# Score products of two heads in turn on two row strips of TensorE, with every engine's order rewritten, in a fused cross-attention and expert-layer kernel

## What is computed

```
h   = x + attention(layernorm(x), ctx, ctx)      # 16 heads of 8 features
out = h + ffn(layernorm(h))
scores = Q K^T / sqrt(8) + slope[head] * softplus(1000 + |i - j|);  softmax over j
ffn(y) = silu(y Sg) * (y Su) Sd  +  sum over the top 2 of 16 experts of  p_e * (silu(y Wg_e) * (y Wu_e)) Wd_e
```

## Time and profile before

| | us |
|---|---|
| median of three runs | 236.87 (236.17 to 238.17) |
| the profiled execution | 235.97 |
| its span, first to last instruction | 234.2 |
| between the two | 1.8 |

### The profile page before, as it was taken

One profiled execution on the slowest core, in us unless ns is written; L12 is line 12 of the kernel. 1 busy time (PEld: TensorE's weight loads), 2 busy tenths in 40 slices (PEclk: granted clock), 3 DMA queues, 4 the chain that ended last, 5 costly groups with the idle time before them and its releaser, 6 DMA issues.

```text
span 234.2 us, 6086 instructions
## 1 busy us (share of the span) xinstructions
PE 213.8 (91%) x1942; PEld 175.4 (75%) x1942; DVE 175.9 (75%) x612; ACT 118.3 (51%) x283; POOL 74.4 (32%) x178
## 2 busy tenths in 40 slices
PE   2969787979999999999999999999999899989995
PEld 2757455757788787977897878878897779768884
DVE  4599636995699678985899569957985788653891
ACT  8565656466426734475346443663367234763310
POOL 2500016010860159013921094107700580038000
PEclk9999999999999999999999999999999999999999
DMA  5553586223312470317032612325123600250000
GB/s 157 175 90 105 125 215 205 80 69 99 87 48 60 83 172 3 104 52 199 3 102 49 157 44 60 84 78 131 38 70 88 165 0 4 84 126 0 1 25 22
DMA packets 13079, 20.24 MB, mean 86 GB/s; under 512 B 2800, under 2 KB 9440, under 8 KB 12544
## 3 DMA queue, kind: packets, MB, share of 16 engines
q1 hardware_dynamic: 12080, 18.64, 31.2%
q10 hardware_dynamic: 976, 1.32, 1.8%
HBM read 16.03 MB, written 3.78 MB: 85 GB/s over the span
## 4 chain that ended last, share of the span: by engine, by line
issue 33%; PE 31%; DVE 17%; POOL 11%; ACT 3%; DMA 1%; DVEq 1%; ACTq 0%; POOLq 0%; SPq 0%
POOL hid L1314 6%; DVE nmax L971 6%; PE ps_up L511 5%; PE ps_pv L444 4%; PE ps_m L537 4%; PE ps_st L425 3%; PE ps_pv L451 3%; PE ps_up L516 2%; DVE tg L1075 2%; DVE stacks_sb L1202 1%; PE ps_up L308 1%; DMA ident<-in_c_ident 1%; DVE hid L1081 1%; PE ps_m L466 1%; POOL ve L1278 1%
## 5 line engine op out<-in xcount | busy, mean ns | idle before, releaser
L791 ACT ACTIVATE th<-ps_up 128x256 f32<-128x256 f32 x72 | 27.6, 383 | 35.5 <-PE ps_up L516 34.8
L735 ACT ACTIVATE probs<-ps_st 128x512 f32<-128x512 f32 x64 | 37.0, 595 | 16.3 <-PE ps_st L425 11.1
L537 PE MATMUL ps_m<-wd_sb,hid 128*128 128x128 f32 x288 | 44.8, 283 | 0.0
L971 DVE TENSOR_REDUCE nmax<-ps_s 128x4 f32<-128x512 f32 x64 | 41.9, 680 | 0.4 <-issue 0.4
L1075 DVE SCALAR_TENSOR_TENSOR tg<-th,ps_up 128x256 f32<-128x256 f32 x72 | 29.8, 414 | 13.5 <-ACT th L791 13.2
L1314 POOL TENSOR_TENSOR hid<-hid,crep 128x256 f32<-128x256 f32 x56 | 39.1, 732 | 0.2 <-issue 0.2
L537 PEld LDWEIGHTS ps_m<-wd_sb,hid 128*128 128x128 f32 x288 | 37.6, 191 | 1.0
L1081 DVE TENSOR_TENSOR hid<-tg,ps_up 128x256 f32<-128x256 f32 x72 | 29.7, 413 | 1.0
L511 PE MATMUL ps_up<-x_hi,wg_hi 128*128 128x256 f32 x72 | 26.6, 369 | 0.4 <-ACT x_hi L772 0.2
L1278 POOL TENSOR_TENSOR ve<-mv,eps_sb 128x1 f32<-128x1 f32 x16 | 3.0, 191 | 69.5 <-DVE mv L1022 69.5
L425 PE MATMUL ps_st<-stacks_sb 98*128 98x128 f16 x256 | 24.8, 220 | 0.2
(11 more groups left out here) (147 smaller groups left out, 434.2 us busy)
## 6 DMA issues: line engine op xcount, KB each, us to landing
crep<-cw_dram SPq DMA_DIRECT2D x28, 256.0 KB, 4.6
stacks_sb<-qk_dram SPq DMA_DIRECT2D x32, 128.0 KB, 3.4
qk_dram<-qk_parts SPq DMA_DIRECT2D x16, 128.0 KB, 1.8
out_y<-x_all SPq DMA_DIRECT2D x8, 128.0 KB, 4.6
wg_sb<-in_wgT ACTq DMA_DIRECT2D x1, 576.0 KB, 3.5
wu_sb<-in_wuT ACTq DMA_DIRECT2D x1, 576.0 KB, 3.3
wd_sb<-in_wd SPq DMA_DIRECT2D x1, 576.0 KB, 4.1
x_all<-in_x SPq DMA_DIRECT2D x2, 256.0 KB, 4.2
```

The source lines that it names most:

```text
L537: last = mm(ps_dn[:, b * P:(b + 1) * P], hid[:, buf, c, b * P:(b + 1) * P], wd_sb[:, c, :], start=(c == 0 and b == 0), stop=(c == SHARED), ...
L735: fn(probs[:, b, g * HG * P:(g + 1) * HG * P], scores_bank(a, g)[:], ACT.Exp).then_inc(exp_sb, 1)
L791: fn(th[:, c % 2, :], ps_up[c % 2][:, 0, :], ACT.Tanh, scale=0.5).then_inc(tanh_sb, 1)
L971: v.tensor_reduce(nmax[:, b, HG * g:HG * g + HG], ps_s[g % 2][:].rearrange("p (h j) -> p h j", h=HG), AX_X, ALU.max, negate=True).then_inc ...
```

## The change

- The stacks are laid out in two strips of 64 rows: heads 0 to 7 at row 0, heads 8 to 15 at row 64, each with 32 rows of features and, in the query stack, two rows of shifts (K: ones). Products take 32 or 34 rows from row 0 or row 64.
- `scores` and `scores_T` take a tuple of groups. i = 0 and 2 are heads 0 to 7, i = 1 and 3 are heads 8 to 15 (ORDER gives the group of heads: 0, 2, 1, 3). With two groups the products alternate between strips and banks, eight in a block. `first` passes single groups.
- In each step after the first attention, the biases of i = 0 and i = 2 of both halves come from SBUF: one copied by ACT, three by DVE (`seed(a, 1, 0)`, `seed(a, 0, 1)`, `seed(a, 1, 1)`). i = 1 computes its one bias product, i = 3 has none.
- SyncE issues the shift rows, two DMAs in place of one of ACT's, in order with its parts and stacks. The stacks are read with eight DMAs of half the size, in place of four. The zero fills of the stacks are gone, the `select` and `cwT_r` fills move to GpSimd.
- PE in a step: scores(0,(0,1)), q, k, down 0, down 1, expert_in_T, scores(0,(2,3)), down 2, up 0, down 3, up 1, scores(1,(0,1)), shift_T 0, router, up 2, scores(1,(2,3)), down 4, up 3, down 5, down 6, scores_T(0,(0,1)), up 4, shift_T 1, down 7, scores_T(0,(2,3)), up 5, down 8, weights_T, weigh_values 0, scores_T(1,(0,1)), up 6, values_T 0, scores_T(1,(2,3)), up 7, attention_T 0, weigh_values 1, and on as before.
- DVE in a step: row_max(0,0), (0,1), gate 8, hidden 8 of f - 1, x2_low, both qk_low, row_max(0,2), (0,3), max_high, max_low, gate 0, hidden 0, row_max(1,0), (1,1), gate 1, hidden 1, router_max, router_shift, gate 2, hidden 2, row_max(1,2), (1,3), max_high, route 0, max_low, route 1, seed(1,0), route 2, gate 3, route 3, hidden 3, route 4, norm1_stats, route 5, 6, seed(0,1), gate 4, norm1_mean, hidden 4, gate 5, hidden 5, seed(1,1), residual2, row_sums 0, normalise 0, gate 6, norm1, hidden 6, and on as before. In `first`, both qk_low stand after the second maximum of half 1 instead of behind the fourth.
- ACT in a step: as before to tanh 3, then exponential(0,0), (0,1), shift_copy 1, tanh 4, exponential(0,2), (0,3), tanh 5, weights_copy, values_copy 0, exponential(1,0), (1,1), tanh 6, exponential(1,2), (1,3), tanh 7, attention_copy 0, values_copy 1, and on as before.
- SyncE in a step: write_parts, shift_rows 0 (the other way round for group 0), stack_k, shift_rows 1, stack_q, then as before.
- `keep_clock` in `first`: 5 and 4 in place of 3 and 3 around scores(0,1,2).

The diff, cut to its core (context and the orders told above are left out):

```diff
@@ -39,9 +39,11 @@
+STRIP = 64
-ZROWS = 96
-AROWS = ZROWS + 2
+AROWS = SROWS + 2
+HS = H // 2
+ORDER = (0, 2, 1, 3)
...
@@ -112,13 +114,13 @@
-        stacks_sb = sb("stacks_sb", [AROWS, 2, 2, H, T], F16)
+        stacks_sb = sb("stacks_sb", [STRIP + AROWS, 2, 2, HS, T], F16)
-        nsplit = sb("nsplit", [P, NB, 2, H], F16)
+        nsplit = sb("nsplit", [P, NB, 2, 2, HS], F16)
...
@@ -223,23 +225,28 @@
-                    sp.wait_ge(act_pads, 1)
-                    sp.wait_ge(dve_pads, 2)
+            def stack_k(p, buf):
-                    src = bass.AP(qk_dram.tensor, (buf * 5 + plane) * (P * T), [[H * T, 2 * DH], [1, H * T]])
-                    sp.dma_start(stacks_sb[row:row + 2 * DH, buf, 1].rearrange("r h t -> r (h t)"), src).then_inc(s_stack, 16)
-                    sp.wait_ge(dve_pads, 1)
+                    for s in range(2):
+                        src = bass.AP(qk_dram.tensor, ((buf * 5 + plane) * P + s * HS) * T, [[H * T, 2 * DH], [1, HS * T]])
+                        at = STRIP * s + row
+                        sp.dma_start(stacks_sb[at:at + 2 * DH, buf, 1].rearrange("r h t -> r (h t)"), src).then_inc(s_stack, 16)
+            def stack_q(p, buf):
-                if not at_start(p):
-                    sp.wait_ge(s_nm[1], 16 * p)
-                    src = bass.AP(qk_dram.tensor, buf * 5 * (P * T), [[H * T, 2 * DH], [1, H * T]])
-                    sp.dma_start(stacks_sb[row:row + 2 * DH, buf, 0].rearrange("r h t -> r (h t)"), src).then_inc(s_stack, 16)
+                    for s in range(2):
+                        src = bass.AP(qk_dram.tensor, (buf * 5 * P + s * HS) * T, [[H * T, 2 * DH], [1, HS * T]])
+                        at = STRIP * s + row
+                        sp.dma_start(stacks_sb[at:at + 2 * DH, buf, 0].rearrange("r h t -> r (h t)"), src).then_inc(s_stack, 16)
+            def shift_rows(a, b, buf):
+                sp.wait_ge(nm_sb, 2 * a + b + 1)
+                for s in range(2):
+                    sp.dma_start(qs[buf][STRIP * s + SROWS:STRIP * s + AROWS, :, b * P:(b + 1) * P],
+                                 nmT[H * s:H * (s + 1), b, :]).then_inc(s_nm[b], 16)
...
@@ -257,24 +264,28 @@
             def load_more():
-                sp.wait_ge(s_nm[0], 16)
-                sp.wait_ge(s_nm[1], 16)
+                sp.wait_ge(s_nm[0], 32)
+                sp.wait_ge(s_nm[1], 32)
             def load_rest():
-                sp.wait_ge(s_stack, 128)
+                sp.wait_ge(s_stack, 256)
-                sp.wait_ge(dve_pads, 3)
+                sp.wait_ge(pool_pads, 2)
             def step(f, a, p, q, abuf):
-                if p is not None:
-                    stacks(p, 1 - abuf)
-                if a is not None and at_start(a): load_more()
+                if at_start(a): shift_rows(a, 0, abuf)
+                if p is not None: write_parts(p, 1 - abuf)
+                if not at_start(a): shift_rows(a, 0, abuf)
+                if p is not None: stack_k(p, 1 - abuf)
+                shift_rows(a, 1, abuf)
+                if p is not None: stack_q(p, 1 - abuf)
+                if at_start(a): load_more()
...
@@ -341,39 +354,36 @@
-            def scores(a, b, g, buf):
-                bank, n = ps_s[g % 2], 2 * NHG * a + NHG * b + g
-                if b == 0 and g == 0:
-                    pe.wait_ge(s_stack, 64 * a + 64)
+            def scores(a, b, groups, buf):
+                n = 2 * NHG * a + NHG * b
+                if b == 0 and 0 in groups:
+                    pe.wait_ge(s_stack, 128 * a + 128)
-                        pe.wait_ge(dve_pads, 1)
-                        pe.wait_ge(act_pads, 1)
-                    elif isinstance(a, int) and a == 1:
-                        pe.wait_ge(act_pads, 3)
-                elif b == 0 and g == 1:
+                if b == 0 and 1 in groups:
-                else:
-                    pe.wait_ge(max_sb, n - 1)
-                if g == 0:
-                    mm(bank[:], dist16[:], slope_hi[:, 0:HG, :], start=True, stop=False, skip_group_check=True)
-                for h in range(HG * g, HG * g + HG):
-                    o = (h - HG * g) * P
-                    last = mm(bank[:, o:o + P], qs[buf][0:ZROWS, h, b * P:(b + 1) * P],
-                              ks[buf][0:ZROWS, h, b * P:(b + 1) * P],
-                              start=(g > 0), stop=True, skip_group_check=True)
-                last.then_inc(s_mm, 1)
+                if b > 0 or groups[-1] > 1:
+                    pe.wait_ge(max_sb, n + groups[-1] - 1)
+                if 0 in groups:
+                    mm(ps_s[0][:], dist16[:], slope_hi[:, 0:HG, :], start=True, stop=False, skip_group_check=True)
+                for k in range(HG):
+                    for i in groups:
+                        row, h = STRIP * (i % 2), HG * (i // 2) + k
+                        last = mm(ps_s[i % 2][:, k * P:(k + 1) * P], qs[buf][row:row + SROWS, h, b * P:(b + 1) * P],
+                                  ks[buf][row:row + SROWS, h, b * P:(b + 1) * P], start=(i > 0), stop=True,
+                                  skip_group_check=True)
+                        if k == HG - 1:
+                            last.then_inc(s_mm, 1)
             def shift_T(a, b):
-                nc.tensor.transpose(ps_nm, nsplit[:, b, :, :].rearrange("p s h -> p (s h)"), ident16[:]).then_inc(nm_mm, 1)
+                nc.tensor.transpose(ps_nm, nsplit[:, b].rearrange("p t s h -> p (t s h)"), ident16[:]).then_inc(nm_mm, 1)
...
@@ -400,32 +410,38 @@
-            def scores_T(a, b, g, buf, f=None):
-                bank, n = scores_bank(a, g), 2 * NHG * a + NHG * b + g
-                seeded = not at_start(a) and (b, g) in ((0, 0), (1, 0), (1, 1))
+            def scores_T(a, b, groups, buf, f=None):
+                n = 2 * NHG * a + NHG * b
+                seeded = {i: not at_start(a) and i % 2 == 0 for i in groups}
-                if at_start(a) and (b, g) == (0, 1):
+                if at_start(a) and b == 0 and 1 in groups:
-                if seeded and b == 0:
-                    pe.wait_ge(seed0_sb, a)
-                elif seeded:
-                    pe.wait_ge(seed1_sb, 2 * a + g - 1)
-                elif not (at_start(a) and b == 0 and g < 2):
-                    pe.wait_ge(exp_sb, n - 1)
-                if g == 0:
-                    pe.wait_ge(s_nm[b], 16 * a + 16)
+                for i in groups:
+                    if seeded[i] and b == 0 and i == 0:
+                        pe.wait_ge(seed0_sb, a)
+                    elif seeded[i]:
+                        pe.wait_ge(seed1_sb, 3 * (a - 1) + 2 * b + i // 2)
+                if not (at_start(a) and b == 0 and groups[-1] < 2):
+                    pe.wait_ge(exp_sb, n + groups[-1] - 1)
+                if 0 in groups:
+                    pe.wait_ge(s_nm[b], 32 * a + 32)
-                first = False if seeded else bias(bank, g)[0]
-                for h in range(HG * g, HG * g + HG):
-                    o = (h - HG * g) * P
-                    last = mm(bank[:, o:o + P], ks[buf][:, h, b * P:(b + 1) * P], qs[buf][:, h, b * P:(b + 1) * P],
-                              start=first, stop=True, skip_group_check=True)
-                    first = False
-                last.then_inc(st_mm, 1)
+                    elif isinstance(a, int) and a == 1:
+                        pe.wait_ge(act_pads, 4)
+                first = {i: False if seeded[i] else bias(scores_bank(a, i), ORDER[i])[0] for i in groups}
+                for k in range(HG):
+                    for i in groups:
+                        row, h = STRIP * (i % 2), HG * (i // 2) + k
+                        last = mm(scores_bank(a, i)[:, k * P:(k + 1) * P], ks[buf][row:row + AROWS, h, b * P:(b + 1) * P],
+                                  qs[buf][row:row + AROWS, h, b * P:(b + 1) * P], start=first[i], stop=True,
+                                  skip_group_check=True)
+                        first[i] = False
+                        if k == HG - 1:
+                            last.then_inc(st_mm, 1)
...
@@ -740,10 +749,6 @@
-            def shift_rows(a, b, buf):
-                act.wait_ge(nm_sb, 2 * a + b + 1)
-                act.dma_start(qs[buf][ZROWS:AROWS, :, b * P:(b + 1) * P], nmT[:, b, :]).then_inc(s_nm[b], 16)
...
@@ -859,10 +860,8 @@
-            fill(stacks_sb[:, 0, 1], zero)
-            act.wait_ge(act_pads, 1)
-            act.wait_ge(dve_pads, 1)
-            fill(ks[0][ZROWS:AROWS], ones16)
+            for s in range(2):
+                fill(ks[0][STRIP * s + SROWS:STRIP * s + AROWS], ones16)
...
@@ -966,28 +965,30 @@
-            def row_max(a, b, g):
-                dve.wait_ge(s_mm, 2 * NHG * a + NHG * b + g + 1)
-                v.tensor_reduce(nmax[:, b, HG * g:HG * g + HG], ps_s[g % 2][:].rearrange("p (h j) -> p h j", h=HG), AX_X, ALU.max,
+            def row_max(a, b, i):
+                g = ORDER[i]
+                dve.wait_ge(s_mm, 2 * NHG * a + NHG * b + i + 1)
```

(14 more changed lines are left out.)

154 lines of the change are left out of this document (70 added, 84 removed).

## The result

| | before | after |
|---|---|---|
| median, us | 236.52 (236.0 to 238.17, four runs) | 248.72 (246.57 to 249.68, four runs) |
| the profiled execution | 235.97 | 246.57 |
| its span | 234.2 | 244.8 |
| PE's mean granted clock | 0.999 (the profiled execution) | 0.986, 0.979, 0.972, 0.972 (all four) |

What follows compares the result with a forecast made beforehand. PE, busy 91%, decides, with short waits mostly on DVE or ACT. Start-up +0.9, first step +0.8, middle steps +2.5, last +0.4 make +4.6 on 235.97: 240.6, predicted as 241.0; range 233.5 to 246, the forecast's own 237.5 to 244.5.

Steps and rivals of the forecast that it cites:

- the middle steps: Five middle pipelined steps: new orders and waits cost +0.5 us each, +2.5 in all.
- the start-up: First attention: half 1's shift rows land late behind SyncE's stack_k issues, +0.9 us, bounds 0 and +1.5.
- (a) to (c): PE work per middle step: strip pairs -1.66, shape switches +1.32, weight loads +0.30, fewer bias products -0.38; sum -0.42 us.
- points 1 to 7: Hand schedule of a middle step under the new orders, with PE's waits on other engines, summing to 25.46 us.
- point 5: Middle step: weights_T at T+15.70, ACT's 0.37 us copy at 16.13, weigh_values waiting for it until 16.55, before T+16.36.
- First step +0.8: First pipelined step: first L444 block 0.15 later and the same longer chain behind it, +0.8 us.
- rest +0.4: Last pipelined step, behind the middle ones: +0.4 us.
- A: Rival: reordered waits stay as large as before and PE's work decides, -0.42 a step, 233.1 us; chance 0.22.
- B: Rival: strips don't overlap, +1.66 us PE work a step over the forecast's, about half in waits, 247 us; chance 0.08.
- D: Rival: row strips switch free, at most -2.04 us a step, -14 in all, 222.6 us; chance 0.03.
- C: Rival: the steps' waits cost what PE saves, only the start-up's +0.9 is left, 237.8 us; chance 0.15.

Runs made afterwards that it cites:

- e3: Kernel after without strips: before's full-height stacks, zero fills and one shift DMA a half, all new orders and four seeds kept; 248.08 us, ratio 1.048.
- e4: Kernel before with score products taken from 64 rows instead of 96, giving them the strip shape without pairs; 242.20 us, ratio 1.024.
- e6: Kernel before with the bias of head group 1 of half 0 copied by ACT instead of computed by PE; 236.93 us, ratio 1.0005.
- e12: e3's kernel with e7's order, first attention's shift rows issued by ACT, shift_T(0,1) between the first two groups as before; 243.47 us, ratio 1.028.
- e5: Kernel before with the shift rows issued by SyncE at the change's places, one DMA each; 242.15 us, ratio 1.021.
- e14: Kernel after with e1's SyncE order, e7's order, and e13's DVE order and clock transposes in the first attention; 242.70 us, ratio 1.025.
- e1: Kernel after; in the first attention SyncE issues half 1's shift rows before stack_k, PE does shift_T(0,1) before the second scores_T group; 247.12 us, ratio 1.044.
- e10: Kernel after with keep_clock(14), transposes that compute nothing, ahead of scores_T(0, 0, (2,)) in the first attention; 247.88 us, ratio 1.041.
- e2: Kernel after with the loops of scores and scores_T exchanged: four products on one strip, then four on the other; 248.86 us.
- e13: e12's kernel with DVE's first-attention order as before (qk_low behind the last row maxima) and before's clock transposes; 240.33 us, ratio 1.017.
- e7: Kernel after with scores_T(1,(0,1)) ahead of weigh_values(0) on PE and exponential(1,0) ahead of values_copy(0) on ACT; 244.63 us, ratio 1.034.
- e8: Kernel after with the third seed written by ACT, and the routing weights' transposes and copy moved earlier; 245.84 us, ratio 1.038.
- e9: Kernel after with the first attention's shift rows issued by ACT, two DMAs a half; 248.26 us, ratio 1.047.
- e11: Kernel after with the changes of e7, e8 and e9 together; 248.48 us, ratio 1.048.

## Why the prediction was wrong

The direction and the main mechanism (waits made by the new orders) were right; the sum was 7.7 us short of the median. Two of its terms failed by 2.7 us each, the middle steps (+2.5 taken, +5.25 measured) and the start-up (+0.9 taken, +3.62 measured), and the granted clock was in no term. By its steps:

**PE's work, (a) to (c).** From windows, PE's busy time in a quick step went from 24.32 to 23.62, so -0.70, where I had -0.42. e3 splits it: 24.32 to 23.95 is the fourth seed, -0.37 (I had -0.38), and 23.95 to 23.62 the strips, -0.33 (I had -0.04). A pair costs as much as one product, as taken from L494 (pairs start 0.056 apart). The switches were priced too high: 13 of them are 1.09 in e4, where the same arithmetic gives 1.6. This error made the forecast too slow, if anything, by 0.3 us a step at most: e3 against after shows 0.33 us of PE work reach the time in full, e6 shows 0.25 reach it not at all.

**Waits, points 1 to 7.** The hand schedule held. Of the step that starts at 117.68, predicted and measured:

| | predicted, T+ | measured, T+ |
|---|---|---|
| scores(1,(0,1)) | 6.40 | 6.38 |
| seed(1,0) starts | 12.85 | 12.83 |
| up 5 | 14.53 | 14.49 |
| cw | 15.28 | 15.26 |
| weights_T | 15.70 | 15.75 |
| weigh_values 0 | 16.55 | 16.87 |
| from it to weigh_values 1 | 4.77 | 4.66 |
| from there to the end | 4.14 | 4.14 |
| step | 25.46 | 25.67 |

The one miss is point 5: the copy of cwT began 0.5 after the transposes (133.43 to 133.93), and weigh_values 0.25 behind its end.

**The sum was mis-sized where I chose.** "25.46 us, against a mean of 24.96. I take +0.5" set a schedule of the quick kind against the mean of both kinds. The quick kind was 24.65, so the schedule itself said +0.8, which I had named only as a bound. Measured is +1.05 a step, 5.25 instead of 2.5: 1.55 us from this choice, 1.05 from the 0.21 by which the schedule fell short of the measured step, the rest from the other kind of step.

**Start-up: +0.9 taken, 3.62 measured.** I had the second issue of half 1's shift rows at 26.3 and its landing at 28.4. It was issued at 27.56 and landed at 29.28. The step that failed is the time of SyncE's issues, not the 2 us from issue to landing, which were 1.72. Three things made them late. The stack reads wait for the second write of the parts (23.47 here, 24.68), 1.7 us behind it; I counted the 1.7 from the first, 0.44 earlier. SyncE's two issues of half 0's rows end at 22.92 and hold back the parts, which leave at 23.03 where ACT's issue lets them go at 22.62 (e12): 0.4. And the two shift issues are 0.65 apart, not 0.3. In after the stack packets have all ended (27.92) before the shift rows' packets run (28.16 to 28.29, 28.82 to 28.95), so there the reads cost time on SyncE and not on the DMA engines; in the full-height kernels, with packets of 8 KB, they cost it on the DMA engines (e5, e12). The move of `qk_low` has no run of its own on the strips. e14, with it moved back, has half 1's products 0.53 later than e1 with the same order on SyncE (28.75 for 28.22), as the writes of the parts then leave later and the rows behind them.

So half 1's products start 1.89 later (29.37 for 27.48), where I had 0.9. The rest is the clock: the wait of 1.66 let it fall, and from these products to the first step are 8.91 us before (27.48 to 36.39), 10.64 after (29.37 to 40.01). e10 takes 1.26 of that 1.73 back. The same wait gave a low stretch of 6.8 us in e2, whose start is the same program: 29.04 to 40.85, 11.81 us.

**The clock was in no term and in no rival.** A stretch of 3.4 us at the 1.2 GHz level takes 0.007 off the mean clock, so after's four runs had two, three, four and four by estimate. From 0.986 to 0.972 the time goes from 246.57 to 249.5, so some 1.5 us for a stretch. The profiled execution, with two, was the fastest of the four; the one or two more of the others are about the 2.15 us that the median lies above it.

**First step +0.8, rest +0.4.** Measured 1.16 and 0.57. Without a drop the first step took 24.27 in e13, 0.35 more than before, and 24.82 in e3, 0.90 more; so the orders' part was about what I had or less. The rest lies with the drop at 47.88, which no run separates.

**The rivals.** A (PE's work decides) fell with the result, and e6, which takes PE work away from the kernel before and gains nothing, speaks against it too. B and D: strips overlap, and their switches are not free. C saw the start-up, but the waits of the steps were not paid by what PE saved: idle time in a quick step rose from 0.33 to 2.05, and busy time fell by 0.70. That is the whole +1.02.

**Still open.** Why the strip kernels lose their clock in the steps. In the profiled executions no kernel of full height did so between the start and the end of the pipelined steps (before, e3, e4, e5, e6, e12, e13), while all of the strips did (after, e1, e2, e7, e8, e9, e10, e11, e14). e3 against after differs in little else. But it is no strict division: executions without a trace had mean clocks of 0.973 (e3) and 0.978 (e12) at full height, as low as after's (in which stage is not on record), and 0.993 with strips (e2, e10). Nor is a drop tied to one wait: PE was busy for 3.08 of the 3.88 us ahead of the drop at 47.88. No run here takes this apart. No version tried beats the kernel before.

## What to carry to other kernels

Split a step into busy and idle time of the deciding engine before and after: here PE's work fell by 0.70 and its waits rose by 1.72, and a step in which the engine is busy 97% of the time still gained nothing when 1% of its work was taken away, as the waits for another engine grew by as much (e6). When a hand-made schedule is compared with a measured step, compare the same kind of step. And when an issue moves, follow it twice: when its new issuer is free for it (each issue took 0.4 to 0.6 us here), and what else is on the DMA engines when it lands. A small transfer that PE waits for belongs ahead of the bulk ones, and a wait of a us or more in a start-up can have a second price, the clock.

## What the runs showed of the hardware

- Two row strips run side by side without being issued in turn: in e2 four products of the second strip are issued behind four of the first, and still start 13 ns behind their partners, ahead of products that were issued before them; the block of eight takes 0.34 us, in turn 0.33.
- A change of strip shape costs 1.09 / 13 = 0.08 us of PE's time with what it uncovers (e4).
- The small shift transfer took 4.0 us from issue to landing (25.17 to 29.16, e12) behind stack reads in packets of 8 KB issued from 0.4 us earlier on by another engine; where these came later it took 1.9 (to 26.65, e13). Behind four stack reads in packets of 4 KB that had just ended it took 1.7 (after).
- In the first attention the granted clock fell to 1.2 GHz within or shortly after waits of PE of 1.11, 1.64, 1.66, 1.75, 2.27 and 3.75 us (e1, e14, after, e12, e3, e5), the last for 6.8 us instead of 3.4, and did not with waits of 1.07 and 0.47 (e13). The same wait of 1.66 led to 3.4 us in after and 6.8 in e2. A stretch of 3.4 us cost 1.3 (after against e10), some 1.5 (after's executions) and 2.0 us (e14 against e7).
- Filling part of such a wait with transposes held the clock there (e10), but in the first step that followed it stood low for 10.2 us instead of 3.4.
